# The last step of sixteen batched triangular inverses, on one 64 x 64 block in place of 128 rows with zeros

## The chip, the cores and the metric

The kernel runs on one core of one Trainium2 chip. The metric is the device time of one execution in microseconds (us). Three runs of the kernel before gave 1859.85 us as median (1858.15 to 1862.78). All data are float32, apart from a few bfloat16 pieces that play no part here.

## The reference, cut to what matters

A model of four layers is applied to four batch elements of 1024 tokens by 128 features. Each layer has an attention of its own and a feed-forward part: layer 0 a linear attention with decay and a mixture of experts, layer 1 a four-layer stack of causal linear attention with GELU blocks and a mixture of experts, layer 2 a delta rule with chunks and an expert, layer 3 a gated delta rule and an expert. Layers 2 and 3 are where the change lies. In both, for every chunk of 128 tokens, the update of a state needs the inverse of a lower triangular matrix with ones on its diagonal:

```
A      = strictly lower part of (beta_i * k_i . k_j [* decay])     128 x 128, one per chunk
T      = (I + A)^-1                                                computed by the kernel as X
v_new  = T (beta * v) - (T (beta * decay * k)) S
```

There are 8 chunks per element, and the kernel inverts four chunks at a time. So there are 4 elements x 2 layers x 2 groups = 16 batched inversions, each of four 128 x 128 matrices.

## The kernel before, in words

**Layout.** Each batch element has its own SBUF arena (`arena0` to `arena3`) and two PSUM banks of 128 x 512 float32 that it takes in turn. The profile calls all arenas `arena` and all banks `ps`. Constants lie in `cst`: the identity, a mask `neg(n)` for each doubling step, and columns `ODD + n`, `EVEN + n` that tell whether the block of 2^n rows to which a row belongs is odd or even.

**Order.** Every engine has a generator per element (`l2_pe(b)`, `l2_act(b)`, ...), which yields between steps, and one of four long strings `TURNS["pe"]`, `["dve"]`, `["act"]`, `["pool"]` says which element takes the next step on that engine (digit 4 is common work). The strings were written by something outside this file and hold for the whole kernel, layer 0 to the end. Each engine works through its own instruction stream strictly in that order, so an instruction that waits holds up all that stands behind it on that engine, of all four elements. Semaphore waits between engines are made by keys: `pe.up(b, "inv_f", ...)` marks, `at("inv_f", ...)` waits. SP issues the DMAs in its own order; the change touches none.

**The inverse.** It is built by doubling. After step n, the diagonal blocks of 2^(n+1) rows are inverted. X4 (128 x 4 x 128) holds the columns of the inverse found so far, G4 (128 x 4 x 192) the matrix still to be worked on, in a compact form, and in its columns 128 onwards the right-hand side r. Each of the seven steps (n = 0 to 6) has these parts:

- `inv_pe` (L1746): four transposes of G4 into a bank (`inv_f`, L1754; the helper's line in the profile is L89), later four matmuls of the masked transposes Y with a stretch of G4 (`inv_p`, L1765; helper's line L86).
- `inv_dve` (L1790): Y = transposed bank x mask `neg(n)`, on 128 x 512 numbers (L1798; helper's line L103).
- `inv_pool` (L1802): r = X x odd mask, and X = X x even mask (L1814, L1816; helper's line L103), on 128 x 4w numbers with w = 2^n.
- `inv_act` (L1769): copies of the result into G4 (`inv_v`, L1780) and X4 (`inv_c`, L1782) for n < 6; in the last step one copy into X4, columns 64 to 127 (`inv_x`, L1786; helper's line L97).

In the last step (n = 6) the odd block is rows 64 to 127 and the even one rows 0 to 63. Only one 64 x 64 block of each mask has anything but zeros beside the diagonal, yet all parts run over 128 rows.

The four transposes are written as four instructions and show as four records in the profile. A float32 matmul shows as two weight loads and two matmul records, so the four matmuls of a step are eight records. After the inverse, `l2_pe` and `l3_pe` go on with the chunks one by one and need `inv_x`.

```
            for i in range(4):
                ins = pe.mm(ps[:, 128*i : 128*i + hi - lo], m.Y[:, col4(i)], m.G4[:, i, lo:hi])
```

With n = 6, lo is 128 and hi 192, so the moving operand is r with 64 columns, over 128 rows, and the weights are 128 x 128.

Of the kernel before, what the change touches and what calls it, by code (L numbers as in the profile page):

```python
# [369 lines left out]
class Ffn3:  # L370
    def __init__(self, room):
# [9 lines left out]
    "pe": ("0123440000000100011000111000111230002111200022110032013000111220001123300103221100133231112223332221"  # L381
           "1122110213332221033002211233300303332221333222111213331001220033300301012002102202233110001130103013"
           "3001100103032300111212211311331100010010010022020033203103322323322000222022020220022020200322001112"
           "2112212212211212211233300331331330331102233100223110123300031122110023100200223320100120001000202110"
           "2300300022000130131133000110003000310113302100300300122200110111221110301020022323001300110111333323"
           "1223112221222033002000102001221022111222213211012333220022100113322112200210001112212223333221022100"
           "1023113303321122113223331311312232231112330331331100310320322022333223223332300131123311332233221331"
           "1132210322103311100233133233002223211001001231331330233003300032232331331332333113223311000201131012"
           "0010310002200033022111022002002111332322003001113302213221022300112000133000211123301211222032001003"
           "2223002003101111131113302330100032233322010311000111122032211332130033001311300332001112203111102221"  # L390
           "0002221102111313112333132233312213122002201102113011201322333322213331123002210101230023322333220032"
           "3322231120011320103322233320313313001100020220011231123323301103130010332200032000312333013111221010"
           "0221100100330033023130112002111200011000112330133122223320112111220330120001100013233220312221122022"
           "1100120001113331233322333122000130221112221103110033003010002333212301332223111112022113000332103332"
           "2233322111301101122111220023003312333232221133223022011202012230022123322200332331112331131002220021"
           "3013300330011003300331103221101300130300330000332020200200133311011000112032331132233223133030030010"
           "2211010011101112212230300330002000122330112221120221121100330000100233220231223112211122000211120002"
           "2100022203332221021100033302113223312211132122232331333113231133122322111220100223010301120011133300"
           "1113321332222321211122313333233332322222213113312211332112110222233000000332232200200020000322033033"
           "3000220000110033300031100001110000011000110000100001111000110031133033311310003303000111000010000111"  # L400
           "3221333003111221133113313311222332233222001221221110021112221121112102313113313100111333222033322223"
           "2033022202222203311122202222120122233222233303333223322233313113332222113333323322232222033330223330"
           "3113033301133003330223333220333311002331330220101330012001012001021021021002121233233213231001100213"
           "0102113101312211302130132102231120123120122311023023023022320230233220311301100331010310300313322123"
           "2013021230133200130130320331200101201201201211233123312121133211312110231001322132001123213221312321"
           "0320322003200320131123022033202311002323133113131131213322033221313300031132032320202221202031133211"
           "0332210133331013330331301330120122012201201210312201330132033203100100020103310211023001110230120201"
           "3012300120311203012103210300120310230112231021022002132132103211000122301001223312002132333110223023"
           "2132330111032110312022302320321013320230312203103230332203213200232100031202301330120102300133321323"
           "1032012013032102132001132012031121032130213210322132221130022321032103120312203120320113321312331231"  # L410
           "3221321123130233002130021322130213200123233233233303303303111300311032102211202222003331313213233211"
           "1221213311323323322333"),
    "dve": ("0000000000000000044141411111212441100011111221122232322332233111223322230333333330000014000001222111"
           "1033300001111100000111120100000112111202200002001000321021022111233133132222201131002000002010022200"
           "0001003111333441231311332322221313103330210110110111013112111222311311333222223030333202000221112313"
           "2021333212202212221231223222223322111010133232023232323333333333333330010033301330310023232322233311"
           "2121313100010002031023200220220202020320112212122112123300030313003011002030000000000000000000223113"
           "3120000123000200023010000010002000121101101100001111311111111200202202022222322222222201101100000300"
           "3010101011330010000000221010111122001131010100002231001320212321101103123212222102121213020200330033"
           "2333030121233113333303330222201102221221211121202233220100033111121120222021102020122232213101323231"  # L420
           "3121102023231133330001221221331221313331111232311333323313132312123110000032302330022223300223332323"
           "2321131113333332222233313131211130202313103333111200200200000330032323222000003101131131133331113003"
           "0000333322323223332222233333311111111113333300011202011202222222100001100110002201022020101200001111"
           "2222333333333300011210102122220133333333233201010002001122203301103301020121022101220000132232300303"
           "1310112112020131333330010000121213322223030101011111030312213131331010330002121311220303110101010131"
           "2123222223000002212121111221313133331212133222211111232323302002000002001113131213332332222331312111"
           "3322000003000200223320023333222003322232032323111111101110302030333322223330303001001111111110003112"
           "1122222223223333000113000031313100331200203031333022222212201111221022010000101100130303330333331111"
           "2002000112002212001010101132033233223322333133111211203302000021121210103130202022220312121111130203"
           "2312123131333310000123322222001013111122030303212030121213100033133020312132220113113022030132210202"  # L430
           "0003232331331121232222331313111121132121010020020023000333333223222213111132332222203202002220000000"
           "0332332330023222111111313111330222220030001113113113301110330000011303030301103311000031001313331000"
           "3000222022222022000031313111130301000331333122222222221103103223033000333003312211100110110201021201"
           "0200223001333300202101022220111133323323312020233000021100102121322030220132323121111120202000113210"
           "2022102201010223232020200013333111113223222311223131232121323233233111131132222221313231311221000300"
           "0003001331211123302001000001003121213132222300300000301001000001110023232333332223322222333320000000"
           "3033300000000012112112332112111121211222111111300030303031111111110101101203221222221112200111111113"
           "3331331111111102222222222002232222322303232222221221101121222212122110230022222222100101333330310333"
           "3031000013333300000000000000010022021222112222333333333300333333332332333333331333333333133233333333"
           "3333333100002101033333030300313032323022220120223332231113211111111111111131133122221103222222222222"  # L440
           "2222230230032230311120221230012112131133210222030033333313333333033320130021002001023312333300113233"
           "0300103301110030210021113021321220112312021211310223220233021122320013113131110111322010033322120232"
# [2586 lines left out]
```

## Time and profile before

| what | value |
|---|---|
| median of 3 runs | 1859.85 us (1858.15 to 1862.78) |
| the profiled execution's own time | 1858.92 us |
| its span, first to last instruction | 1857.1 us |
| mean granted TensorE clock | 0.994 of full |
| busy: PE, weight loads, VectorE, ScalarE, GpSimd | 1768.9, 1340.9, 1238.0, 1091.2, 1273.5 us |
| span less busy PE | 88.2 us |

The profile is of one execution. PE is TensorE's matmul side, PEld its weight loads, DVE VectorE, ACT ScalarE, POOL GpSimd. The time of a matmul record runs to its modelled end, so records of one stream overlap: four records of 0.27 us each can be done in 0.6 us. What a stream costs is therefore read from the starts: from the first record of a group to the first of what comes after it.

### The profile page before, as it was taken

The page shows a single profiled execution, that of the slowest core. Times are in us where ns is not written, and L with a number is a line of the kernel's source. Part 1 is how long each engine was busy: PE and PEld are TensorE (multiplying, and loading weights), DVE is VectorE, ACT ScalarE, POOL GpSimd, SP SyncE. Part 2 cuts the span into 40 slices and gives each one's busy share as a digit, 9 for nine tenths or more (in the row PEclk, how much of TensorE's full clock was granted, in tenths as well). Part 3 has the DMA queues.
Part 4 walks back from the last instruction along what each step waited for, and adds up shares of the span by engine and source line. Part 5 has one row for each costly group of instructions (what it writes and reads, how often), then busy time and mean ns, then how long its engine had stood idle before and what let it go on. Part 6 is the DMA issues. An engine that isn't in the chain of part 4 may idle for free.

```text
span 1857.1 us, 31831 instructions
## 1 busy us (share of the span) xinstructions
PE 1768.9 (95%) x10270; PEld 1340.9 (72%) x10270; DVE 1238.0 (67%) x4307; ACT 1091.2 (59%) x2684; POOL 1273.5 (69%) x1779
## 2 busy tenths in 40 slices
PE   8999999989999999999999899999999999999998
PEld 5788998665666567657665577777778887888874
DVE  7953235687769876887789655543466756768774
ACT  6563225656886578667876676564345556544456
POOL 6665558998879987997899884341356755554465
PEclk9999999999999999999999999999999999999999
DMA  6200000010000000000000000000000001000002
GB/s 237 77 11 1 1 2 4 1 47 1 1 1 1 1 1 1 1 1 1 1 1 1 5 5 5 1 7 1 2 4 1 1 23 26 18 1 1 1 7 63
DMA packets 24473, 26.44 MB, mean 14 GB/s; under 512 B 3492, under 2 KB 21284, under 8 KB 23924
## 3 DMA queue, kind: packets, MB, share of 16 engines
q1 hardware_dynamic: 24308, 24.41, 4.1%
q8 instruction: 83, 1.36, 0.3%
q14 instruction: 82, 0.67, 0.1%
HBM read 22.26 MB, written 2.15 MB: 13 GB/s over the span
## 4 chain that ended last, share of the span: by engine, by line
PE 69%; POOL 14%; DVE 7%; ACT 5%; issue 4%; DMA 0%; POOLq 0%; SPq 0%; DVEq 0%; ACTq 0%
PE ps L86 63%; POOL arena L103 13%; PE ps L89 6%; ACT arena L97 4%; DVE arena L103 2%; DVE arena L109 1%; DVE arena L106 1%; POOL arena L106 1%; DVE arena L126 1%; DVE arena L141 1%; ACT L97 1%; DVE arena L123 0%; DVE arena L129 0%; DVE arena L112 0%; ACT arena L98 0%
## 5 line engine op out<-in xcount | busy, mean ns | idle before, releaser
L103 POOL TENSOR_TENSOR arena<-arena 128x512 f32<-128x512 f32 (+6 forms) x796 | 734.5, 937 | 298.9 <-DVE arena L103 146.5
L97 ACT ACTIVATE arena<-ps 128x128 f32<-128x128 f32 (+9 forms) x1100 | 368.6, 369 | 445.1 <-PE ps L86 337.8
L86 PE MATMUL ps<-arena 128*128 128x128 f32 (+4 forms) x2864 | 465.1, 296 | 25.8 <-DVE arena L103 12.8
L86 PEld LDWEIGHTS ps<-arena 128*128 128x128 f32 x2864 | 380.0, 192 | 118.0 <-issue 47.5
L103 DVE TENSOR_TENSOR arena<-ps,arena 128x128 f32<-128x128 f32 (+4 forms) x680 | 295.0, 446 | 239.3 <-PE ps L86 227.4
L97 ACT ACTIVATE arena<-arena 128x128 f32<-128x128 f32 (+1 forms) x772 | 300.0, 442 | 45.8 <-POOL arena L103 41.3
L97 ACT ACTIVATE arena<-ps,cols 128x512 f32<-128x512 f32 x324 | 216.9, 689 | 170.2 <-PE ps L86 158.1
L86 PE MATMUL ps<-arena,cst 128*128 128x360 f32 (+1 forms) x768 | 294.0, 498 | 17.4 <-POOL arena L103 7.3
L86 PE MATMUL ps<-arena,moe 128*128 128x256 f32 (+1 forms) x960 | 289.8, 441 | 1.4 <-DVE arena L109 0.4
L89 PE MATMUL ps<-cst,arena 128*128 128x128 f32 x1392 | 239.6, 274 | 15.4 <-ACT arena L97 5.1
L103 POOL TENSOR_TENSOR arena<-arena,cst 128x144 f32<-128x144 f32 (+7 forms) x320 | 138.3, 435 | 142.6 <-ACT arena L97 96.6
L109 DVE SCALAR_TENSOR_TENSOR arena<-ps,arena 128x128 f32<-128x128 f32 (+2 forms) x424 | 141.4, 372 | 132.2 <-PE ps L86 104.1
L89 PEld LDWEIGHTS ps<-cst,arena 128*128 128x128 f32 x1392 | 169.0, 142 | 75.6 <-issue 30.4
L86 PEld LDWEIGHTS ps<-moe,arena 128*128 128x128 f32 x1728 | 203.5, 192 | 23.5 <-issue 21.2
L86 PEld LDWEIGHTS ps<-arena,moe 128*128 128x128 f32 x960 | 173.3, 191 | 55.7 <-issue 29.2
L86 PEld LDWEIGHTS ps<-arena,cst 128*128 128x128 f32 x768 | 133.9, 192 | 100.6 <-issue 44.4
L86 PE MATMUL ps<-moe,arena 128*128 128x128 f32 x1728 | 204.7, 275 | 0.0
L141 DVE TENSOR_REDUCE arena<-arena 128x144 f32<-128x1152 f32 (+1 forms) x136 | 173.0, 1277 | 17.1 <-POOL arena L103 14.3
L103 POOL TENSOR_TENSOR arena<-arena,rows 128x512 f32<-128x512 f32 (+1 forms) x140 | 151.5, 1083 | 11.3 <-PE ps L89 5.3
L103 POOL TENSOR_TENSOR arena<-arena,mhalf 128x4 f32<-128x4 f32 (+1 forms) x136 | 151.2, 1111 | 11.3
L126 DVE BATCH_NORM_STATS2 arena<-arena 128x6 f32<-128x128 f32 x544 | 140.1, 271 | 16.6 <-POOL arena L103 9.0
L86 PE MATMUL ps<-arena,wf 128*128 128x512 f32 x256 | 127.3, 596 | 0.8 <-ACT arena L97 0.5
(109 smaller groups left out, 1897.6 us busy)
## 6 DMA issues: line engine op xcount, KB each, us to landing
rows<-in_rows SPq DMA_DIRECT2D x1, 2253.0 KB, 15.4
arena<-in_x SPq DMA_DIRECT2D x8, 256.0 KB, 5.0
wf<-in_wf SPq DMA_DIRECT2D x2, 1024.0 KB, 6.5
arena<-in_L_ffn_W SPq DMA_DIRECT2D x8, 256.0 KB, 3.1
out_dram<-arena SPq DMA_DIRECT2D x8, 256.0 KB, 2.5
wmod<-in_wmod SPq DMA_DIRECT2D x4, 384.0 KB, 9.0
arena<-kept SPq DMA_DIRECT2D x24, 64.0 KB, 3.0
arena<-kept SPq DMA_DIRECT2D x8, 192.0 KB, 3.0
```

The costliest lines, as they stand in the source:

```text
L86: return UNSENT if self.e is None else self.e.matmul(out, lhsT, rhs, start=start, stop=stop)
L89: return UNSENT if self.e is None else self.e.transpose(out, in_, ident)
L97: return self.e.activation(out, in_, func, bias=bias, scale=scale)
L103: return UNSENT if self.e is None else self.e.tensor_tensor(out, a, c, op)
L106: return UNSENT if self.e is None else self.e.tensor_scalar(out, a, s1, s2, op0, op1)
L109: return UNSENT if self.e is None else self.e.scalar_tensor_tensor(out, a, s, c, op0, op1)
L126: return UNSENT if self.e is None else self.e.bn_stats(out, a)
L141: return UNSENT if self.e is None else self.e.tensor_reduce(out, a, AX.X, ALU.add)
```

## The change

In the last step alone: the transposes take rows 0 to 63 of G4 (64 rows, 128 columns, against a 64 x 64 identity), and give 64 columns each. VectorE negates the 64 x 256 block that they leave in rows 64 to 127 rather than masking 128 x 512. The matmuls take 64 x 64 weights and a 64 x 64 moving operand, both in rows 64 to 127, and write rows 0 to 63 of the bank. The right-hand side is no longer a product with the odd mask on GpSimd but a copy on ScalarE of rows 64 to 127 of X4, columns 0 to 63 to columns 64 to 127, right behind the copies of step 5; it waits for ScalarE's own last instruction and for GpSimd's second product of step 5. GpSimd's product with the even mask stays, and now waits for that copy. The last copy takes 64 rows. All four strings of TURNS are replaced by others of the same lengths with the same number of each digit (3122, 3842, 2031 and 1066 digits; PE's from its 45th digit on, and in 1855 places).

```diff
 TURNS = {
-    "pe": ("0123440000000100011000111000111230002111200022110032013000111220001123300103221100133231112223332221"
...
-    "pool": ("4102304011002300112003110022110001133001110022442200112233011002112233011332211333122133223300222233"
...
+    "pool": ("4102304011002300112003110022110001133001110022440022113301122000112221133113333322001223333122332200"
...
         def inv_pe(b, m, *key):
...
                 for i in range(4):
-                    ins = pe.tr(ps[:, col4(i)], m.G4[:, i, 0:128] if n else m.tri[:, col4(i)], ident)
+                    if n < 6:
+                        ins = pe.tr(ps[:, col4(i)], m.G4[:, i, 0:128] if n else m.tri[:, col4(i)], ident)
+                    else:
+                        ins = pe.tr(ps[:, 64 * i:64 * i + 64], m.G4[0:64, i, 0:128], ident[0:64, 0:64])
...
-                lo, hi = (w, 128 + w) if n < 6 else (128, 192)
-                for i in range(4):
-                    ins = pe.mm(ps[:, 128 * i:128 * i + hi - lo], m.Y[:, col4(i)], m.G4[:, i, lo:hi])
+                for i in range(4):
+                    if n < 6:
+                        ins = pe.mm(ps[:, col4(i)], m.Y[:, col4(i)], m.G4[:, i, w:128 + w])
+                    else:
+                        ins = pe.mm(ps[0:64, 64 * i:64 * i + 64], m.Y[64:128, 64 * i:64 * i + 64],
+                                    m.X4[64:128, i, 64:128])
...
         def inv_act(b, m, *key):
...
+                    if n == 5:
+                        act.wait_ge(*act.last(b))
+                        act.wait_ge(*at("inv_k", b, 5, *key))
+                        act.act(m.X4[64:128, :, 64:128], m.X4[64:128, :, 0:64]).then_inc(
+                            *act.up(b, "inv_r", b, 6, *key))
                 else:
                     act.wait_ge(*at("inv_k", b, 6, *key))
-                    act.act(m.X4[:, :, 64:128], ps[:, :, 0:64]).then_inc(
+                    last = bank[0:64, 0:256].rearrange("p (t n) -> p t n", n=64)
+                    act.act(m.X4[0:64, :, 64:128], last).then_inc(
                         *act.up(b, "inv_x", b, *key, free=(b, "inv_p", n, *key)))
...
         def inv_dve(b, m, *key):
...
-                dve.tt(four(m.Y), four(ps[:, :]), over(neg(n)), ALU.mult).then_inc(
-                    *dve.up(b, "inv_y", b, n, *key, free=(b, "inv_f", n, *key)))
+                if n < 6:
+                    ins = dve.tt(four(m.Y), four(ps[:, :]), over(neg(n)), ALU.mult)
+                else:
+                    ins = dve.ts(m.Y[64:128, 0:256], ps[64:128, 0:256], -1.0, None, ALU.mult)
+                ins.then_inc(*dve.up(b, "inv_y", b, n, *key, free=(b, "inv_f", n, *key)))
...
         def inv_pool(b, m, *key):
...
-                    pool.tt(r, xc, odd, ALU.mult).then_inc(*pool.up(b, "inv_r", b, n, *key))
-                    pool.wait_ge(*pool.last(b))
+                    if n < 6:
+                        pool.tt(r, xc, odd, ALU.mult).then_inc(*pool.up(b, "inv_r", b, n, *key))
+                        pool.wait_ge(*pool.last(b))
+                    else:
+                        pool.wait_ge(*at("inv_r", b, n, *key))
                     pool.tt(xc, xc, even, ALU.mult).then_inc(*pool.up(b, "inv_k", b, n, *key))
```

## Rows read from the trace of the kernel before

**Rows 1.** The page: span, busy time of each engine, and the chain that ended last.

```profile
span 1857.1 us, 31831 instructions
PE 1768.9 (95%) x10270; PEld 1340.9 (72%) x10270; DVE 1238.0 (67%) x4307; ACT 1091.2 (59%) x2684; POOL 1273.5 (69%) x1779
PE 69%; POOL 14%; DVE 7%; ACT 5%; issue 4%; DMA 0%; POOLq 0%; SPq 0%; DVEq 0%; ACTq 0%
```

**Rows 2.** Busy time by stretch; the first inversion's last step is at 1359.8 us.

```profile
core 0: us, PE busy (x) PEld busy (x) DVE busy (x) ACT busy (x) POOL busy (x), PEclk, DMA share, GB/s
0.00:350.00 350.00, 334.45 (x2027) 283.43 (x2027) 188.30 (x756) 159.90 (x299) 230.63 (x312) 1.00 0.13 44
350.00:1320.00 970.00, 928.27 (x4683) 637.12 (x4682) 687.60 (x2266) 647.06 (x1573) 738.99 (x889) 0.99 0.01 4
1320.00:1560.00 240.00, 228.20 (x1682) 195.79 (x1681) 151.35 (x540) 127.30 (x389) 146.45 (x285) 1.00 0.04 10
1560.00:1790.00 230.00, 222.97 (x1642) 191.59 (x1641) 176.48 (x624) 116.46 (x348) 114.89 (x246) 1.00 0.02 5
```

**Rows 3.** Groups of instructions, shapes kept apart (columns in the first line).

```profile
line engine op names shapes xcount | busy us, mean ns | idle before us <-releasers
L86 PE MATMUL ps<-arena 128*128 128x64 f32 x128 | 16.5, 272 | 1.1 <-POOL arena L103 0.7 <-issue 0.4
L103 DVE TENSOR_TENSOR arena<-ps,cst 128x512 f32<-128x512 f32 x104 | 70.7, 684 | 34.9 <-PE ps L89 33.3
L103 DVE TENSOR_TENSOR arena<-ps,arena 128x256 f32<-128x256 f32 x32 | 13.4, 421 | 63.4 <-PE ps L86 60.4 <-ACT arena L97 2.9
L103 POOL TENSOR_TENSOR arena<-arena,cst 128x256 f32<-128x256 f32 x32 | 19.9, 621 | 15.2 <-ACT arena L97 13.9
L97 ACT ACTIVATE arena<-arena 128x256 f32<-128x256 f32 x128 | 53.6, 419 | 0.4
L86 PEld LDWEIGHTS ps<-arena 128*128 128x128 f32 x2864 | 380.0, 192 | 118.0 <-issue 47.5 <-DVE arena L103 29.8 <-ACT arena L97 14.3
L86 PEld LDWEIGHTS ps<-sm,arena 128*1 128x1 f32 x24 | 0.9, 81 | 1.7 <-issue 1.3
```

**Rows 4.** Timeline around one last step: start us, us, what, count, idle before.

```profile
1522.39 0.55 ACT L97 ACTIVATE arena<-ps 128x256 f32<-128x256 f32 x2
...
1523.02 1.31 POOL L103 TENSOR_TENSOR arena<-arena,cst 128x256 f32<-128x256 f32 x2 [0.67 <-ACT arena L97]
...
1523.22 0.60 PE L89 MATMUL ps<-cst,arena 128*128 128x128 f32 x4
...
1523.66 1.02 PE L86 MATMUL ps<-arena 128*128 128x512 f32 x2
1523.86 0.69 DVE L103 TENSOR_TENSOR arena<-ps,cst 128x512 f32<-128x512 f32 x1 [3.06 <-PE ps L89]
...
1524.52 0.38 PE L86 MATMUL ps<-sm,arena 128*128 128x128 f32 x2
```

**Rows 5.** Timeline of TensorE alone around a last step and a matmul on 64 rows.

```profile
1359.82 1.00 PE L86 MATMUL ps<-arena 128*128 128x64 f32 x8
1360.76 1.12 PE L86 MATMUL ps<-wmod,arena 64*128 64x512 f32 x2
1361.81 1.12 PE L86 MATMUL ps<-arena,moe 128*128 128x512 f32 x2
```

**Rows 6.** Timeline of TensorE alone around four transposes of one row.

```profile
1569.18 0.59 PE L86 MATMUL ps<-arena 128*128 128x512 f32 x1
1569.70 0.40 PE L89 MATMUL ps<-cst,arena 1*128 1x1 f32 x4
1570.03 0.70 PE L86 MATMUL ps<-arena 128*128 128x512 f32 x1
```

**Rows 7.** L86 from 1304.9 to 1306.4: durations ns min/median/max, first and last start us.

```profile
L86 PEld LDWEIGHTS ps<-wmod,arena x2: 183/184/186, 1305.2 to 1305.3; 64*128 64x128 f32 x2
L86 PE MATMUL ps<-wmod,arena x2: 589/641/693, 1305.2 to 1305.7; 64*128 64x512 f32 x2
L86 PE MATMUL ps<-arena,moe x1: 697/697/697, 1306.3 to 1306.3; 128*128 128x512 f32 x1
```

**Rows 8.** The chain of waits in order of time: start us, us, what.

```profile
1482.38 0.23 POOL arena L106
1482.60 0.59 POOL arena L103
1483.19 0.14 issue
1483.33 1.08 PE ps L86 x8
```

**Rows 9.** Who waited for whom from 1350 to 1790 us: total, times, longest us.

```profile
PEld ps L86 <- ACT arena L97: 12.5, 29, 0.9
```

More of the change, by code:

```diff
@@ L380 @@
 TURNS = {
-    "pe": ("0123440000000100011000111000111230002111200022110032013000111220001123300103221100133231112223332221"
[L382 to L412, printed above, removed]
@@ new lines @@
+    "pe": ("0123440000000100011000111000111230002111200011220031023000111220001123300102221100132221113333332221"
+           "1122110133010023003330222331132220333003330221203332220012011333002200131100233002221100301313300100"
+           "1100130311223200020200200300300300113323221110011001001010010011011001233223233003221112212212212212"
+           "2122112112101333223323322332332322322023211233002211011000321121220013300200223201100120001000202110"
+           "2300300022000130131133001100000300310113301002300013022200110111221110300120022323001300110111333323"
+           "1223112221222332011210011002212201000112232210333210330201122001122111100100033131131122222333333023"
+           "3322132211100023213220133323311233221113221311220322123330033023303220221231122233111233313332111223"
+           "0220220312203111313300233003323222230033133313010332130221003100330330133233312213212330011302110210"
+           "0110322000100033022122011022000111332322003001113302213220122300112000330111002133221011222132032220"
+           "0332000101100110113113323322103223330000103110001110111223122330200333001133002100112201122113321322"
+           "2101120001113132113012233322313311322112211201110003203301223332221122233300231013012330023323223002"
+           "3322232110011320103322233320133313001000201220011232330331121103130330032200012000321333011223111022"
+           "1001100100330033021330112020111211000110002133022331222110331112220012330011001000332132231122200020"
+           "0322233020001133110233112332100222022210003020011011131113232321333333221211311112032211330002133303"
+           "3321223112221122211032111330333002333030221222311101330222020110013331321332212200020030112221021003"
+           "0002113033300322220111303310301010030033003303312211333112220112011030020233000202332233133030030010"
+           "2211100011101331102212020330002331220002220112112210211100330002012233200122312302221110121001100020"
+           "1002202223222031300021013311323223312211132122231332113113331333111300100012031221311322233222110011"
+           "1200133111213322322222233323332333223221211112122211311332022332233333000000222200200020000220032200"
+           "0133033000330033000310001100100031100031001001110030001000111001010003330000333030001100001132133300"
+           "2113122111122211112121113322330022332330220133111021111001111222012022022112121131122313333311122331"
+           "3322212222211222122221212221122220220112230333320222323332332223332332223330333223011333330333101333"
+           "3031331302231002333212033331331333013333002203333201201002331021021021002102012010021121331211331210"
+           "0132211003231201220101133102132131102302230230230320322023011231120132210330313033003130130133010022"
+           "3102231320233102130013021031233012002012110210210212113321332121332112211302100211321003221321232103"
+           "2203023023200223111023112032032031331310031222311332211313130113300023002323023322323230032210220111"
+           "3331103300120313313022333133031033102102210210101022100100012301021033310231300211302101121033012012"
+           "0013110230210201323102300123012302201132022023100213121201223110003010231232012313300123331122302302"
+           "1323110331210321031220202302311230233022303103132032201332203123120030002210310231332010320133300233"
+           "1203020233021021300230210230123023112322122230211200321031030210320130221321123113123312333213220113"
+           "2100301320321332103003123112231312331231321320132032033003030303310031112221212211223333131321332112"
+           "1122213311323323322333"),
@@ new lines @@
+    "pool": ("4102304011002300112003110022110001133001110022440022113301122000112221133113333322001223333122332200"
+           "0202033023320011330000101011122003300000011100101010010101222223303032331122122122121121332233232332"
+           "2231123300220110012012032031201020121130122101103103301203321200221231013203132331201233231032133310"
+           "1231230002231321332120321332032133201132312223130003200310321330321131011220201220130230123302130103"
+           "3221031031021310213002103212310212311103203213320030222001310320112312011333010301220231022310210120"
+           "1333013320230212013210031203132312032123111032332010013020022210311013211030013332012032230102013012"
+           "2201201333021332012200102313210231221330132011123000231230300002202103013211121321111111222322222223"
+           "0233300300013333330033330333211001112202302200111100223321002132001311203020112211330110322130130223"
+           "0132203302210103321331001332120013231120023021120221133112233122313022323320003311133133023322002010"
+           "3011330101200131122110023220011323230022311300322113330112200330220103302201133001201331221002232100"
+           "233112322312003300322113303221133112200331100332212333221111333322"),
@@ L1776, in inv_act @@
                 w = 2 ** n
-                ps = four(banks.get(b, "inv_p", n, *key)[:, :])
+                bank = banks.get(b, "inv_p", n, *key)
+                ps = four(bank[:, :])
                 act.wait_ge(*at("inv_p", b, n, *key))
```

130 lines of the change are left out of this document (60 added, 70 removed).

## The prediction

> **What bounds the kernel now.** I read the page first. TensorE is busy for 1768.9 of 1857.1 us, and 69% of the chain that ended last is its own work, against 14% for GpSimd and 7% for VectorE [rows 1]. So 88.2 us at most is TensorE's open idle time, and a change counts if it alters what TensorE has to stream, or how it waits. Next I read the stretches: up to 1320 us, where nothing but the order is changed, TensorE is idle for 15.6 + 41.7 = 57.3 us; in the two stretches that hold all sixteen last steps (1320 to 1790 us) it is idle for 11.8 + 7.0 = 18.8 us of 470 [rows 2]. There ScalarE is busy for about half of the time (127.3 of 240, 116.5 of 230), VectorE for 63% and 77%, GpSimd for 61% and 50%: none of them is near its bound. The groups by shape say the same of the step itself: before the 128 records with 64 columns (16 inversions x 4 matmuls x 2 records) TensorE was idle for 1.1 us in all [rows 3]. The other elements' work covers the chain of a step nearly everywhere. So the helpers' savings are nearly free of effect, and the question is what the 64-row instructions cost TensorE.
>
> **What they cost now.** Four transposes start at 1523.22 and the next matmul at 1523.66, so they take 0.44 us, 0.11 each; two records of 512 columns then take 0.86 us, to 1524.52, or 0.43 each [rows 4]. The eight 64-column records start at 1359.82 and what follows at 1360.76. That is 0.94 us, of which 0.09 us belongs to the change to 64 rows (below). A 64-column record streams for 0.43 x 64/512 = 0.054 us, which can't cover a next load of 128 columns as long as 0.11; so some 0.04 falls on what follows, and I take 0.85 + 0.04 = 0.89 us, 0.11 each. A 128-column record costs 0.11 too: the 64-column one is held up by its weight load, not by its streaming.
>
> **Part 1, going to 64 rows and back.** The trace has such instructions. Before two records on 64 rows, the stream loses 0.09 us; those two take 1.05 us to the next start where two on 128 rows take 0.86 [rows 4, 5], and the four transposes on one row start 0.52 us after a 512-column record that otherwise holds 0.43 [rows 6]. Further, the first 64-row record lasts 693 ns against 589 for the second, and the first 128-row record behind them 697 [rows 7]: 0.104 us of weight load that is otherwise hidden stands open on each side. From 1.05 = 0.86 + 0.10 + 0.09, the way back costs 0.09 before the next start. So one visit to fewer rows costs 0.09 + 0.09 us plus the open load of the first record inside, plus that of the first behind.
>
> The Trainium skill (TensorEngine Tiling (Array Packing), Key Properties) says that a change of tiling mode, not of tile, drains TensorE. This speaks against the change. By that rule the trace agrees: 0.09 us on the way in and 0.09 on the way out.
>
> **Part 2, the transposes.** The four on one row take 0.33 us to the next start, with 0.09 on entry [rows 6]. They have 128 weight columns as the new ones will; the new ones stream 64 columns and not one, 0.054 us, which the next load covers but for the last. What follows has its load open, 0.05 us behind a transpose's load and 0.10 behind a matmul's; I take 0.08. Sum: 0.09 + 0.33 + 0.05 + 0.08 = 0.55 us, against 0.44: **+0.11 us**.
>
> **Part 3, the matmuls.** A load of 128 columns lasts 192 ns and one of a single column 81 [rows 3], so 64 columns take (192 - 81) / 2 = 0.056 us; with 0.054 of streaming that gives 0.058 a record if one covers the other. Sum: entry 0.09, first load open 0.05, eight records 0.46, exit 0.09, load behind 0.08: 0.77 us, against 0.89: **-0.12 us**.
>
> Together -0.01 us an inversion, about -0.2 us for all 16. Both ends: if the visits cost nothing, the transposes take 0.33 - 0.09 = 0.24 us [rows 6] and the matmuls 0.46, -0.63 us an inversion, -10.1 us in all. If the visits cost all of the 0.31 each and no record gets shorter, it is +0.62 us, +9.9 us in all. I take the middle because the rows show both the cost and, for short loads, the gain.
>
> **Part 4, the helpers.** VectorE: 0.684 us becomes that of 256 columns out of PSUM, 0.42 by the nearest row [rows 3]: -0.26 x 16 = -4.2 us of VectorE, on the way from transposes to matmuls. In the example the masking ran from 1523.86 to 1524.55 and its bank is free 0.26 us earlier [rows 4]. GpSimd: one product of 0.621 us goes, 16 x 0.62 = -9.9 us. ScalarE: one copy of 256 columns out of SBUF more, 0.419 us [rows 3], 16 x 0.42 = +6.7 us, plus the wait for its own last instruction, between 0 and 0.3 us (the gap between 1522.94, when ScalarE's pair ended, and 1523.02, when GpSimd began, says about 0.1 [rows 4]). The wait for GpSimd's second product of step 5 costs nothing: it stands right behind the first, which the matmuls of step 5 needed. Behind the new copy stand the other elements' ScalarE instructions, each up to 0.5 us later. Who would feel it: weight loads waited 12.5 us for ScalarE in this stretch, 29 times [rows 9]; with ScalarE half idle I put it at +0.3 us, between 0 and 16 x 0.5 = 8.
>
> The copy is ready before the product was: 0.42 + 0.1 us against 0.62. In one inversion this is on the final chain: GpSimd, held by an inverse square root's work, makes the right-hand side from 1482.60 on, and TensorE starts at 1483.33 after an idle 0.7 us [rows 8, 3]. ScalarE would have it earlier. The whole is bounded by the 1.1 us of [rows 3], and I give -1.0 for it. What is late next is the Y block. TensorE's own latency gets shorter, too (-0.3 us from first to last matmul), for which I add -0.3. No DMA moves, and SP's queue stays as it is.
>
> **Part 5, the new order.** All four strings change, in layers 0 and 1 too, where each instruction costs the same as before. Their quality can't be read from the rows. It can be bounded: an order can change TensorE's waits alone, 88.2 us of open idle [rows 1]. A tenth of these each way is 9 us. I take 0 and keep +/-9 for the range.
>
> **The sum.** -0.2 + 0.3 - 1.0 - 0.3 = -1.2 us. The profiled execution took 1858.92 us, so its successor would take 1857.7; that execution was 0.9 us under the median of its runs, so the median I forecast is 1858.6 us. About 0.3% (5.6 us) is what a measurement of this kernel can tell from no change; the forecast is within it.
>
> **The rivals.**
>
> A, faster: the groups on 64 rows often come when TensorE has just waited, or next to one another, so that the visits are free, and every record is shortened. That is the lower end of parts 2 and 3: 1858.9 - 10.1 - 1.3 + 0.3 + 0.9 = 1848.7 us. For it: TensorE was idle before the step in some cases [rows 8]. Against it: the page has TensorE busy 95%, and three of three places in rows 5 to 7 paid.
>
> B, slower: within a group on 64 rows the loads stay open, each matmul record costs 0.056 + 0.054 = 0.11 us as now, each transpose as well, and the visits come on top. That is +0.62 x 16 = +9.9 - 1.0 + 0.9 = 1868.7 us. It decides from 0.41 us an inversion upwards (5.6 + 1.0 over 16). For it: nothing in the trace has 64 weight columns on 64 rows. Against it: the second 64-row load began at 1305.3, while the first matmul of 0.69 us from 1305.2 ran, and the second one lasted 589 ns, no longer than hidden loads make it [rows 7].
>
> The Trainium skill (TensorE: Matmul & The Clock Gate, Part 3: Packing small matmuls) has a rule that weight loads overlap matmuls in flight only when they go to another row group. By that rule B would hold, 1868.7 us; the trace does not agree, since the second load on the same 64 rows ran inside the first matmul.
>
> C, the order: the new strings leave TensorE a tenth more or fewer waits, +/-9 us, 1849.6 or 1867.6 us. The unchanged stretch to 1320 us would show it, with its 57.3 us of idle time [rows 2].
>
> D, the change does not do what it says, since the right-hand side still waits for GpSimd: it doesn't, except through the product of step 5, and that was counted.
>
> **How the numbers follow.** The forecast, with C small: 0.44. A, with C of the same sign, past 0.3%: 0.30 (A alone 0.12, the order 0.18). B or a worse order, past 0.3%: 0.26 (B 0.11, the order 0.15). The range runs from A with some of the order, 1846, to B with some, 1871. So faster 0.30, same 0.44, slower 0.26.
>
> **What would show it.** The weight load of 64 columns on 64 rows should last about 137 ns and the eight matmuls 0.6 us from the first start to the last end of streaming; if they take 0.9, B holds. Records behind a visit should be 0.05 to 0.10 us longer. If the stretch without inversions changes by more than 3 us, it was the order, and the forecast was right or wrong by luck. ScalarE should have 16 copies of 64 x 256, about 0.42 us each, and GpSimd 16 fewer products. TensorE's busy time should stay within 3 us of 1768.9. The forecast is wrong if an inversion's two groups cost TensorE over 0.4 us more or less than before.

## The result, and the profile after

The changed kernel took 1868.64 us as median of 11 runs (1863.03 to 1870.88), the kernel before 1858.85 us (1856.87 to 1866.01, 11 runs): ratio 1.0042, with an interval of [1.0029, 1.0056]. It is slower by 0.42%, where 1858.6 us, within 0.3%, was forecast. Run again later on another chip (e9 below) it gave 1.0051 [1.0038, 1.0064].

First the page of the changed kernel, in answer to [rows 1].

```profile
span 1866.0 us, 31841 instructions
PE 1771.9 (95%) x10270; PEld 1340.6 (72%) x10270; DVE 1238.5 (66%) x4307; ACT 1097.5 (59%) x2694; POOL 1266.7 (68%) x1763
```

TensorE's busy time rose by 3.0 us, its open idle time from 88.2 to 1866.0 - 1771.9 = 94.1 us. ScalarE has 6.3 us more in all (forecast 6.7). That is no proof of the forecast, since the new strings also changed how often ScalarE loads an activation table: 82 times in place of 88 on this line, 105.2 us in place of 112.9. The 16 new copies by themselves take 6.6 us. GpSimd has 6.8 us less in all; its products of 128 x 256 with a mask fell from 19.9 to 10.0 us, as forecast.

The groups that the change made, in answer to [rows 3], have the sizes forecast: the load of 64 columns lasts 134 ns (forecast 137), VectorE's instruction 0.428 us (0.42), ScalarE's copy 0.415 us (0.42).

```profile
L86 PE MATMUL ps<-arena 64*64 64x64 f32 x128 | 10.7, 223 | 1.6 <-issue 1.6
L86 PEld LDWEIGHTS ps<-arena 64*64 64x64 f32 x128 | 8.6, 134 | 4.7 <-issue 4.0
L106 DVE TENSOR_SCALAR arena<-ps 64x256 f32<-64x256 f32 x16 | 6.8, 428 | 3.6 <-PE ps L89 3.1
L97 ACT ACTIVATE arena<-arena 64x256 f32<-64x256 f32 x16 | 6.6, 415 | 0.5
L97 ACT ACT_TABLE_LOAD x82 | 105.2, 1283 | 3.3 <-PE ps L86 1.1 <-PEq L3041 0.7
```

TensorE's timeline, in answer to [rows 5, 6], first around the four transposes of one last step:

```profile
1530.18 1.02 PE L86 MATMUL ps<-arena 128*128 128x512 f32 x2
1531.13 0.46 PE L89 MATMUL ps<-cst,arena 64*128 64x64 f32 x4
1531.52 2.90 PE L86 MATMUL ps<-arena 128*128 128x512 f32 x13
```

Two records of 512 columns hold 0.95 us, which is 0.86 + 0.09 for the way in; the four transposes hold 0.39 us with the way out. Then around the eight matmul records of another:

```profile
1756.64 0.49 PE L89 MATMUL ps<-cst,arena 128*128 128x128 f32 x3
1757.06 0.68 PE L86 MATMUL ps<-arena 64*64 64x64 f32 x8
1757.66 0.47 PE L89 MATMUL ps<-cst,arena 64*128 64x64 f32 x4
1758.06 0.71 PE L86 MATMUL ps<-arena 128*128 128x128 f32 x4
```

Eight records hold 0.60 us from their start to the next, and so they do in ten of the sixteen inversions of this trace; in the other six it is 0.65 to 1.37 us, with TensorE idle before what follows in five of them. The first record of 128 rows behind such a group lasts longer, as before the change: the longest below is the 512-column one right behind the matmuls, 697 ns against the usual 0.59 us.

```profile
L86 PE MATMUL ps<-arena x13: 218/218/697, 1531.5 to 1534.1; 64*64 64x64 f32 x8, 128*128 128x512 f32 x4, 128*128 128x128 f32 x1
```

The last term of each sum below is this open load, the two before it are the way in and what the group holds. So the transposes cost 0.09 + 0.39 + 0.10 = 0.58 us (forecast 0.55, before 0.44) and the matmuls 0.09 + 0.60 + 0.10 = 0.79 (0.77, before 0.89): +0.04 us an inversion, +0.6 us in all. At most 0.6 us of the loss is there. By stretch, in answer to [rows 2]:

```profile
0.00:350.00 350.00, 332.67 (x2014) 281.83 (x2015) 192.96 (x754) 158.19 (x293) 228.78 (x308) 0.99 0.13 44
350.00:1320.00 970.00, 931.16 (x4686) 640.69 (x4686) 691.18 (x2290) 647.09 (x1579) 751.64 (x903) 0.99 0.01 4
1320.00:1560.00 240.00, 226.73 (x1675) 192.70 (x1673) 147.51 (x515) 129.69 (x386) 130.94 (x264) 0.99 0.04 10
1560.00:1790.00 230.00, 218.30 (x1607) 184.58 (x1605) 167.86 (x602) 118.86 (x354) 109.02 (x232) 1.00 0.02 5
```

Up to 1320 us little differs: TensorE had made 6710 records before and has made 6700 now. By 1560 us it is 8392 and 8375. Between 1560 and 1790 us TensorE made 1607 where it had made 1642, and was idle for 11.7 us in place of 7.0. These counts cover the same instructions in another sequence, so they only point to the place; the experiments weigh it.

### The profile page after: what moved, and what is told of

Its sections match the earlier page's. It is cut to its first block, busy times and chain, and to the rows that moved or that the text cites. A ratio compares the mean times of both kernels' runs of the same rounds, so it can differ in the third digit from the quotient of the medians.

```text
span 1866.0 us, 31841 instructions
## 1 busy us (share of the span) xinstructions
PE 1771.9 (95%) x10270; PEld 1340.6 (72%) x10270; DVE 1238.5 (66%) x4307; ACT 1097.5 (59%) x2694; POOL 1266.7 (68%) x1763
## 4 chain that ended last, share of the span: by engine, by line
PE 72%; POOL 13%; DVE 7%; issue 4%; ACT 4%; DMA 0%; SPq 0%; POOLq 0%; DVEq 0%; ACTq 0%
PE ps L86 66%; POOL arena L103 12%; PE ps L89 6%; ACT arena L97 3%; DVE arena L103 2%; DVE arena L106 1%; DVE arena L109 1%; POOL arena L106 1%; DVE arena L141 1%; ACT L97 1%; DVE arena L123 0%; DVE arena L126 0%; DMA arena<-in_x 0%; DVE arena L112 0%; SPq L146 0%
## 5 line engine op out<-in xcount | busy, mean ns | idle before, releaser
L97 ACT ACTIVATE arena<-ps 128x128 f32<-128x128 f32 (+12 forms) x1100 | 368.5, 369 | 450.4 <-PE ps L86 338.0
L86 PE MATMUL ps<-arena 128*128 128x128 f32 (+4 forms) x2864 | 458.3, 294 | 25.4 <-DVE arena L103 8.4
L86 PEld LDWEIGHTS ps<-arena 128*128 128x128 f32 (+1 forms) x2864 | 376.2, 189 | 123.3 <-issue 59.2
L97 ACT ACTIVATE arena<-arena 128x128 f32<-128x128 f32 (+3 forms) x788 | 307.8, 444 | 49.6 <-POOL arena L103 45.0
L86 PE MATMUL ps<-arena,cst 128*128 128x360 f32 (+1 forms) x768 | 299.0, 501 | 16.9 <-POOL arena L103 10.4
L86 PE MATMUL ps<-arena,moe 128*128 128x256 f32 (+1 forms) x960 | 289.2, 442 | 1.7 <-DVE arena L103 1.7
L89 PE MATMUL ps<-cst,arena 128*128 128x128 f32 (+1 forms) x1392 | 242.7, 277 | 20.7 <-ACT arena L97 8.5
L89 PEld LDWEIGHTS ps<-cst,arena 128*128 128x128 f32 (+1 forms) x1392 | 168.9, 144 | 84.7 <-issue 36.1
L86 PEld LDWEIGHTS ps<-moe,arena 128*128 128x128 f32 x1728 | 202.9, 192 | 23.0 <-issue 19.9
L86 PEld LDWEIGHTS ps<-arena,moe 128*128 128x128 f32 x960 | 175.2, 192 | 57.1 <-issue 28.6
L86 PE MATMUL ps<-moe,arena 128*128 128x128 f32 x1728 | 204.2, 275 | 0.0
L86 PEld LDWEIGHTS ps<-arena,cst 128*128 128x128 f32 x768 | 133.1, 193 | 95.6 <-issue 50.2
L103 POOL TENSOR_TENSOR arena<-arena,cst 128x144 f32<-128x144 f32 (+7 forms) x304 | 129.7, 429 | 98.6 <-ACT arena L97 70.9
L106 POOL TENSOR_SCALAR arena<-arena 128x4 f32<-128x4 f32 (+1 forms) x264 | 62.2, 236 | 109.0 <-DVE arena L129 73.7
```

Source lines behind the costliest of these rows:

```text
L86: return UNSENT if self.e is None else self.e.matmul(out, lhsT, rhs, start=start, stop=stop)
L89: return UNSENT if self.e is None else self.e.transpose(out, in_, ident)
L97: return self.e.activation(out, in_, func, bias=bias, scale=scale)
L103: return UNSENT if self.e is None else self.e.tensor_tensor(out, a, c, op)
L106: return UNSENT if self.e is None else self.e.tensor_scalar(out, a, s1, s2, op0, op1)
```

## The experiments

Theory S said that the step costs it, by its array shapes and ScalarE's extra work. Theory O said that the new strings of TURNS do. Ratios are to the kernel before on the same chip, with 95% intervals.

**Step and order taken apart.** e1 has the old `inv_*` functions and the new strings, e2 the changed functions and the old strings.

```diff
 # e1: the kernel before
-TURNS = {... the old strings ...}
+TURNS = {... the new strings ...}
 # e2: the changed kernel
-TURNS = {... the new strings ...}
+TURNS = {... the old strings ...}
```

> The old last step (128 rows, product on GpSimd) under the four new strings of TURNS. Theory O (the new order costs it, the step is nearly free): +8 to +10 us on the kernel before, ratio 1.0043 to 1.0054. Theory S (the 64-row step costs it, by its visits to another array shape and ScalarE's extra copy): within 2 us of the kernel before, ratio 0.999 to 1.001. A middle value would say that each has its share, or that an order is good only with the step it was made for.

> The changed last step under the old strings of TURNS. Theory O: the step by itself, counted on the changed trace: transposes 0.575 against 0.44 us, matmuls 0.80 against 0.89 us, so +0.05 us x 16 = +0.8 us of TensorE, and -1.0 us for the earlier right-hand side: within 2 us of the kernel before, ratio 0.999 to 1.001. Theory S: +8 to +10 us, ratio 1.0043 to 1.0054.

Measured: e1 1.0084 [1.0067, 1.0100], median 1876.40 us; e2 0.9991 [0.9979, 1.0002], 1858.49 us beside 1860.92. The step is free under the old order (-1.7 us, not told from nothing). The order costs 15.5 us with the old step and 9.5 to 11 with the changed one (1.0042 and 1.0051 against 0.9991). Theory S falls, and e1 lost more than the 8 to 10 us that theory O had for it. The two aren't additive: the changed step gains 1.7 us under the old order and 6 to 8 under the new.

**Which stretch of the order.** Each engine's string was put together from one order up to the turns that each element had had at a time T in that order's trace, and the other order's remaining turns. (The string of a single engine was not exchanged alone: I expected the engines to wait for one another in a circle. That was not tried on the chip.)

```diff
 # for each engine; done[d] = turns of element d up to T
-TURNS[engine] = new
+TURNS[engine] = (first order's turns up to done[d] of each element) + (second order's turns beyond done[d])
```

> The changed step; the old order of turns up to what had been done at 1340 us, the new order for the rest. By the same amount of TensorE's work done, the changed kernel was 3 us late at 125 us, 1 to 3 us late from there to 1365 us, and 8.5 us at the end. Theory O with the loss in the late part: +6 to +7 us on the kernel before. Theory S: +8 to +10 us here too. If an order's loss is not additive, anything between 0 and 9.

> The changed step; the new order of turns up to what had been done at 1341 us, the old order for the rest. Theory O with additive parts: +2 to +3 us on the kernel before (the early loss alone). Theory S: +8 to +10 us.

> The changed step; the new order of turns up to what had been done at 1560 us in the changed kernel's trace, the old order for the rest. The new order's loss shows in the late half alone and grows in about equal pieces (by the same work done, the changed kernel is 0.9 us late at 1365, 3.1 at 1538, 6.5 at 1757, 8.5 at 1824). Theory P (the loss is piecewise, each stretch of the new order has its own): +2 to +4 us on the kernel before. Theory M (the two orders don't fit each other at a seam, as in the run that changed over at 1340 us the other way): +8 us or more, with the jump right behind 1560 us.

> The changed step; the new order up to what had been done at 1700 us in the changed kernel, the old order behind. Theory L (the new order's loss is made in its last 170 us: by the same work done it is 4.4 us late at 1704, 6.5 at 1757, 8.5 at 1824, and its clock is at half for 13.7 us from 1820 us on against 6.8 before): +3 to +5 us on the kernel before. Theory P (it is made in pieces from 1340 us on): +6 us or more.

> The same with the changeover at 1790 us, so only the order of the end is the old one. Theory L with the loss in the end itself (half clock, elements that finish together): +4 to +6 us. Theory P: +7 to +9 us.

> The changed kernel as it is, beside the runs below on the same chip: +8 to +10 us on the kernel before, ratio 1.0043 to 1.0054. It is the reference for the two changeovers.

| run, all with the changed step | ratio | interval |
|---|---|---|
| e2, old order throughout | 0.9991 | [0.9979, 1.0002] |
| e4, new until 1340 us, then old | 0.9997 | [0.9987, 1.0007] |
| e5, new until 1560 us | 1.0030 | [1.0017, 1.0042] |
| e10, new until 1700 us | 1.0020 | [1.0011, 1.0029] |
| e11, new until 1790 us | 1.0057 | [1.0044, 1.0070] |
| e9, new throughout | 1.0051 | [1.0038, 1.0064] |
| e3, old until 1340 us, then new | 1.0104 | [1.0088, 1.0120] |

The new order costs nothing up to 1340 us, where nothing but the order is changed. Its loss lies behind: against e4 it is 4 to 6 us by 1560 or 1700 us, and another 5 to 7 us by 1790; the last 70 us add nothing. Few of the sizes written down beforehand were met. e10 (3.7 us) fits theory L and e9 fits, but e4 lost nothing where theory O had 2 to 3 us, e5 (5.6 us) lies between theories P and M, and e11 (10.6 us) lies above both L and P: the end by itself, where L had put a part of the loss, has none. e3 was forecast at 0 to 10 us. The changeover is not free: e3 lost 19 us, 10 more than the whole new order. I take it that the new order's late part meets elements that the old order had brought to other places; that is not shown. The pieces are therefore sizes to within a few us and no more, and that e5 stands above e10 is of that kind, or noise.

**What the order's loss hangs on.** e6 gives the right-hand side back to GpSimd under the new order; e7, e8 and e12 try a form on all 128 rows with 64 weight columns.

```diff
 # e6: inv_act without the copy; inv_pool, n == 6
-                        pool.wait_ge(*at("inv_r", b, n, *key))
+                    if n == 6:
+                        r = m.X4[:, :, 64:128]
+                    pool.tt(r, xc, odd, ALU.mult).then_inc(*pool.up(b, "inv_r", b, n, *key))
+                    pool.wait_ge(*pool.last(b))
 # e7 (old order), e8 (new order): all 128 rows
-                        act.act(m.X4[64:128, :, 64:128], m.X4[64:128, :, 0:64]).then_inc(
+                        act.act(m.X4[:, :, 64:128], m.X4[:, :, 0:64], scale=cst[:, ODD + 6:ODD + 7]).then_inc(
-                        ins = pe.tr(ps[:, 64 * i:64 * i + 64], m.G4[0:64, i, 0:128], ident[0:64, 0:64])
+                        ins = pe.tr(ps[:, col4(i)], m.G4[:, i, 0:128], ident)
-                        ins = pe.mm(ps[0:64, 64 * i:64 * i + 64], m.Y[64:128, 64 * i:64 * i + 64],
-                                    m.X4[64:128, i, 64:128])
+                        ins = pe.mm(ps[0:64, 64 * i:64 * i + 64], m.Y[:, 64 * i:64 * i + 64],
+                                    m.X4[:, i, 64:128])
-                    ins = dve.ts(m.Y[64:128, 0:256], ps[64:128, 0:256], -1.0, None, ALU.mult)
+                    ins = dve.ts(m.Y[:, 0:256].rearrange("p (t n) -> p t n", n=64), four(ps[:, :])[:, :, 0:64], -1.0, None, ALU.mult)
 # e12: e7 with e6's product in place of the scaled copy
```

> The new order and the changed step, but the right-hand side made by GpSimd's product with the odd mask (128 x 256, into X4) in place of ScalarE's copy. The old step under the new order lost 15.5 us, the changed one 9.8 (or 8.4): theory G (the new order counts on GpSimd being free and on the early copy): +13 to +17 us. Theory T (it is TensorE's and VectorE's larger work of the old step that costs more under it): +8 to +10 us.

> The old order; a last step that stays on all 128 rows: full transposes, VectorE negates 128 x 256, ScalarE's copy is scaled by the odd mask's column (128 x 256, so rows 0 to 63 are zero), and the matmuls take 64 weight columns on 128 rows. No visit to another array shape. By the measured terms: transposes 0.44 us as before, matmuls eight records of 0.058 = 0.46 against 0.89, so -0.43 x 16 = -6.9 us of TensorE on the kernel before. Theory B (TensorE bounds the late part): -6 to -9 us, ratio 0.995 to 0.997. Theory W (what is saved turns into waits): within 2 us of the changed step under the old order, ratio 0.998 to 1.000.

> The same 128-row form under the new order. Theory V (the new order loses because it was made for 64-row groups that cost less than they do, some 0.6 us an inversion): its loss goes with the visits, so it comes to within 1 us of the same step under the old order. Theory O (it waits elsewhere, whatever the groups cost): it stays 8 us or more behind that run.

> The old order; the 128-row form with 64 weight columns, but with the right-hand side from GpSimd's product in place of ScalarE's copy. Against the run with the copy (ratio 0.9981) it tells what the copy is worth under the old order. Theory C (nothing: GpSimd's product is seldom late, TensorE idled for 1.1 us in all before the last matmuls): ratio 0.997 to 0.999. Theory G (as under the new order, where the product cost 3 to 5 us more than the copy): 1.000 to 1.002.

Measured: e6 1.0071 [1.0056, 1.0087]; e7 0.9981 [0.9971, 0.9992], median 1856.71 us beside 1859.58; e8 1.0032 [1.0020, 1.0045]; e12 0.9992 [0.9981, 1.0004].

Under the new order, the product on GpSimd costs 0.20 to 0.29% more than the copy, 4 to 5 us, as theory G has it; the interval of e6 just overlaps that of e9. Under the old one e12 stands 0.11% above e7, between the ranges of theories C and G and with overlapping intervals: some 2 us or nothing. And e8 stays 0.51% behind e7, 9.5 us: without the transposes' visits the order costs as much as with them. The matmuls of e7 and e8 still pay theirs, as the lines below show, so this test was only half of what it was meant to be; but under the old step, without a visit in any last step, the order cost most (e1, 15.5 us). So theory V falls.

e7 is the only kernel here whose interval shows it faster than the one before. But it saved 3.5 us, not the 6.9 expected, and its timeline says why:

```profile
1361.58 0.94 PE L86 MATMUL ps<-moe,arena 128*128 128x128 f32 x7
1362.45 0.68 PE L86 MATMUL ps<-arena 128*64 128x64 f32 x8
1363.06 1.12 PE L86 MATMUL ps<-wmod,arena 64*128 64x512 f32 x2
```

The seven records before hold 0.87 us where 7 x 0.11 = 0.78 are due, and the eight hold 0.61 us. A matmul on 128 rows with 64 weight columns pays the way in and out just as one on 64 x 64 does. So the 6.9 us were never saved; they didn't turn into waits, as theory W had it. On TensorE, what e7 has over e2 is the visit of the transposes alone, (0.58 - 0.44) x 16 = 2.2 us.

**VectorE.** In the chain of waits the shares of VectorE differ under the two orders. Two answers for 1700 to 1790 us, first e2 (old order), then the changed kernel:

```profile
by line: PE ps L86 67.5%; PE ps L89 21.5%; POOL arena L103 1.9%; ACT arena L97 1.9%; issue 1.8%; DVE arena L106 1.5%; DVE arena L126 1.4%; DVE arena L129 0.9%; DVE arena L103 0.7%; DVE arena L112 0.5%; DVE arena L109 0.4%; POOL arena L106 0
```

```profile
by line: PE ps L86 60.4%; PE ps L89 18.5%; DVE arena L103 4.8%; DVE arena L106 4.4%; DVE arena L123 4.2%; issue 1.9%; ACT arena L97 1.9%; DVE arena L109 1.7%; POOL arena L103 1.0%; DVE arena L112 0.8%; ACT arena L98 0.4%; DVEq L80 0.0%; POO
```

TensorE's own lines fall from 89.0% to 78.9%, VectorE's rise from 5.4% to 15.9%. One place of it, in the changed kernel's chain in order of time:

```profile
1729.11 0.30 DVE arena L103
1729.41 0.07 issue
1729.48 0.46 POOL arena L103
...
1730.02 0.47 POOL arena L103
1730.48 0.04 DVEq L80
1730.52 0.61 DVE arena L109 x3
1731.13 0.25 DVE arena L106
1731.38 0.21 DVE arena L112
1731.59 0.14 issue
1731.73 0.46 PE ps L86 x2
```

Five VectorE instructions of 0.28 to 0.34 us stand one behind the other, the last of them the copy that TensorE waits for, with an idle 1.00 us. e13 and e14 take VectorE work away under each order. They leave out all but 8 of 128 columns of v in layers 2 and 3, so both layers' values are made from what stood there.

```diff
-                    dve.ts(m.vb[:, col4(i)], ps[:, 0:128], m.ng[:, i:i + 1], None, ALU.mult).then_inc(
+                    dve.ts(m.vb[:, 128 * i:128 * i + 8], ps[:, 0:8], m.ng[:, i:i + 1], None, ALU.mult).then_inc(
...
-                    dve.tt(m.vb[:, c], ps[:, 128:256], row("bkvb3", 128, 128), ALU.add).then_inc(
+                    dve.tt(m.vb[:, 128 * i:128 * i + 8], ps[:, 128:136], row("bkvb3", 128, 8), ALU.add).then_inc(
...
-                    dve.ts(m.vb[:, c], m.vb[:, c], m.bt[:, i:i + 1], None, ALU.mult).then_inc(*dve.up(b))
+                    dve.ts(m.vb[:, 128 * i:128 * i + 8], m.vb[:, 128 * i:128 * i + 8], m.bt[:, i:i + 1], None, ALU.mult).then_inc(*dve.up(b))
```

> The changed kernel (new order) with VectorE relieved: of the values v that layers 2 and 3 compute, only 8 of each 128 columns are biased and scaled (three instructions a chunk of 8 columns in place of 128; the rest of v is left as it was in SBUF, so that part of both layers is left out). 96 VectorE instructions get about 0.2 us shorter each, 19 us in all; TensorE's work stays the same. Theory X (under the new order the chain passes through VectorE: 16% of 1700 to 1790 us against 5% before, 30% of 1400 to 1460 against 14%): at least 4 us more of a gain than the same relief gives under the old order; so 1.000 to 1.003. Theory Y (VectorE is only where the chain happens to be; what is missing is the order's own balance): a gain within 2 us of that under the old order; 1.004 or more.

> The same relief under the old order, beside the changed step under the old order (ratio 0.9991). Theory X: VectorE is off the chain here, so 0.997 to 0.999 (0 to 4 us of gain). Theory Y: as large a gain as under the new order, whatever that is.

Measured: e13 1.0031 [1.0019, 1.0043], e14 0.9990 [0.9976, 1.0004]. The same relief gains 0.11 to 0.20% under the new order (against 1.0042 and 1.0051), 2 to 4 us, and 0.01% under the old. Each instruction got some 0.13 us shorter, 12 us in all and not 19. This lies between the two theories, and the interval of e13 overlaps those of the changed kernel. So it is likely, and not shown, that VectorE is a part of what holds TensorE up in the new order; the rest of the loss stayed in any case.

**The clock.** Another part of the loss may be in the granted clock. The changed kernel at its end:

```profile
1806.00:1820.00 14.00, 11.16 (x62) 7.51 (x60) 11.15 (x51) 9.29 (x21) 9.95 (x17) 0.99 0.00 1
1820.00:1834.00 14.00, 11.66 (x44) 7.72 (x44) 3.29 (x26) 12.12 (x26) 8.20 (x9) 0.52 0.15 38
```

Column PEclk is the third from the end: 0.99, then 0.52. For almost all of 14 us TensorE had 1.2 in place of 2.4 GHz, after a stretch in which it was busy for 11.2 of 14 us. Its records are longer there, four transposes of one form before and after the fall:

```profile
1816.44 0.60 PE L89 MATMUL ps<-cst,arena 128*128 128x128 f32 x4
1821.51 1.11 PE L89 MATMUL ps<-cst,arena 128*128 128x128 f32 x4
```

From 1790 to 1840 us the clock of e2 is 0.93 and that of the changed kernel 0.86. First e2, then the changed kernel with one earlier place:

```profile
1790.00:1840.00 50.00, 44.67 (x203) 27.38 (x202) 28.98 (x117) 36.39 (x71) 40.66 (x47) 0.93 0.14 38
```

```profile
1400.00:1460.00 60.00, 50.64 (x412) 46.32 (x411) 41.94 (x127) 34.22 (x125) 40.59 (x86) 0.97 0.00 1
1790.00:1840.00 50.00, 43.76 (x222) 30.30 (x222) 29.67 (x134) 32.91 (x68) 34.70 (x48) 0.86 0.07 17
```

The shares lost, (0.93 - 0.86) x 50 = 3.5 us and (1.00 - 0.97) x 60 = 1.8 us, are full-speed time that TensorE was not granted. As an estimate from these rows, some 5 of the 10 us are clock, if all of it counts.

The runs give a second estimate. Each lists its mean granted clock. Over its runs this was 0.992 to 0.993 for the kernel before and 0.988 for the changed kernel (both times), which is about 14 and 22 us of full-speed time not granted. Among the runs of the kernel before alone, on four chips, 1 us more of it goes with 0.35 to 0.63 us more of time. By that the 8 us are worth 3 to 5 us. But e4 had 0.9905, about 18 us not granted, and its ratio is not told from that of e2. So lost clock doesn't cost the same everywhere, and whether it fell because TensorE had been waiting, or would have cost its time by itself, was not tested.

## Why the prediction was wrong

**Part 1, the visits:** right. 0.09 us on each way and an open load of 0.10 are what the new groups show, and the Trainium skill's rule on draining (TensorEngine Tiling (Array Packing), Key Properties) agrees again. I had taken it for a matter of rows; e7 shows it for weight columns too.

**Parts 2 and 3:** right to 0.03 us each (0.58 and 0.79 against 0.55 and 0.77). Loads within a group on 64 rows are hidden, so rival B falls: eight matmul records hold 0.60 us, and with open loads they would hold 0.9. Rival A falls too: every visit between busy records paid. For the matmuls these are 13 of the 16 ways in; before the other three groups TensorE stood idle.

**Part 4, the helpers:** their sizes are as forecast, and e2 (-1.7 us, not told from nothing) agrees with what parts 1 to 4 gave, -1.2 us. What it missed is that this term depends on the order: 4 to 5 us hang on the early right-hand side under the new one.

**Part 5, the order:** this is the step that failed. I wrote "I take 0 and keep +/-9 for the range". It was worth 9.5 to 11 us with the changed step. That the range held the value (1868.64 within 1871) is luck: it lies past the 1867.6 us that +9 for the order gives, and the upper end came from rival B, which falls, with some of the order on top. Rival C had the mechanism and nearly its size, but I gave worse orders 15% and let the centre stand at zero. C also said that the unchanged stretch to 1320 us would show it. It did not: the order was harmless there (e4) and lost everything behind it, where I had counted only 18.8 us of idle time and called the helpers' savings nearly free of effect. And the bound itself was wrong. "An order can change TensorE's waits alone" leaves out the clock: open idle rose by 5.9 us, but busy time rose as well, by 3.0 us, where the same step under the old order has 1769.4 us of it (e2), 0.5 more than before. Busy time counts the records that a halved clock has stretched, and the mean clock fell from 0.993 to 0.988.

What stays open is what in the new order lets VectorE's work stand in line where it does, and how the loss splits between VectorE (2 to 4 us by e13 and e14, barely told from nothing), the clock (3 to 5, an estimate, and VectorE's share may be partly the same time) and the rest.

## What to carry to other kernels

A change that comes with a new instruction order is two changes: run the step under the old order first, since here the step was free and the order cost 0.5%. An order that is harmless in one stage can cost most in another, so it has to be judged stage by stage. A smaller matmul on part of the array saves nothing near full-size ones unless its group gains more than a visit costs, here 0.09 + 0.09 us for the two ways and 0.05 + 0.10 for the two open loads, 0.33 us for a group of 64-column matmuls. The matmuls gained 0.10 us net of it, the transposes lost 0.14.

## What the runs showed that was not expected

- A float32 matmul with 64 weight columns on all 128 rows pays the switch: the eight records of e7 start 0.09 us late and what follows waits as well. A transpose with 64 weight columns on 128 rows, in the kernel before, did not. Its four records lasted 273 ns on average, where the first one behind a switch has its load open and lasts 0.05 us longer or more:

```profile
L89 PE MATMUL ps<-cst,arena 128*64 128x128 f32 x4 | 1.1, 273 | 0.0
```

One of them starts 0.86 us behind the start of two records of 512 columns, so with no way in, and what follows starts 0.11 us later:

```profile
1222.62 1.02 PE L86 MATMUL ps<-arena,moe 128*128 128x512 f32 x2
1223.48 0.27 PE L89 MATMUL ps<-cst,arena 128*64 128x128 f32 x1
1223.59 0.61 PE L86 MATMUL ps<-moe,arena 128*128 128x128 f32 x4
```

- The same step, with the same instructions, gained 1.7 us under one order and 6 to 8 us under the other. Its worth can't be read from its own rows alone.
- Two orders spliced at 1340 us, up to where neither had lost time, cost 19 us (e3), more than either order alone.
